# The key sums of an attention step issued directly behind its weighted product, ahead of the step's remaining score tiles

## What is computed

```
x = x + attn(layernorm(x))                 # 8 heads, each a difference of two softmaxes
    scores = q @ k.T                       # 16 score heads of width 16, 1024 x 1024 each
    probs  = softmax(scores)
    diff   = probs[even] - lam * probs[odd]
    attn   = rms_scaled(diff @ v) @ Wo.T
x = x + ffn(layernorm(x))                  # gates: sigmoid, sigmoid, tanh; scan over the 16 batches
```

## Time and profile before

| | |
|---|---|
| time, median of 3 runs | 5260.5 us (5259.5 to 5261.4) |
| time of the profiled execution | 5259.74 us |
| its span | 5257.9 us |
| granted TensorE clock, mean | 0.979 |
| TensorE (PE) busy | 4979.5 us, 95% |
| VectorE (DVE) busy | 4021.4 us, 76% |
| GpSimd (POOL) busy | 2891.7 us, 55% |
| ScalarE (ACT) busy | 2722.8 us, 52% |

### The profile page before, as it was taken

One profiled execution on the slowest core, in us unless ns is written; L12 is line 12 of the kernel. 1 busy time (PEld: TensorE's weight loads), 2 busy tenths in 40 slices (PEclk: granted clock), 3 DMA queues, 4 the chain that ended last, 5 costly groups with the idle time before them and its releaser, 6 DMA issues.

```text
span 5257.9 us, 65030 instructions
## 1 busy us (share of the span) xinstructions
PE 4979.5 (95%) x24784; PEld 1695.8 (32%) x24784; DVE 4021.4 (76%) x6183; ACT 2722.8 (52%) x3173; POOL 2891.7 (55%) x2118
## 2 busy tenths in 40 slices
PE   6999999999999999999999999999999999999999
PEld 2224232332423223242332423233242322323237
DVE  6877777877778877777887777787777887777526
ACT  1464645556465554545556454554546555463652
POOL 3573746647275573727657374664727557372750
PEclk7899999999999999999999999999999999999999
DMA  6031221302222131222303122130222213122117
GB/s 141 26 60 46 50 64 37 69 37 58 52 45 69 33 64 40 45 66 51 67 26 62 45 45 69 34 72 37 54 56 45 69 33 61 43 45 59 65 49 280
DMA packets 127706, 311.05 MB, mean 59 GB/s; under 512 B 27297, under 2 KB 30498, under 8 KB 113442
## 3 DMA queue, kind: packets, MB, share of 16 engines
q1 hardware_dynamic: 124178, 289.33, 23.2%
q10 hardware_dynamic: 3216, 17.57, 0.9%
HBM read 172.07 MB, written 99.61 MB: 52 GB/s over the span
## 4 chain that ended last, share of the span: by engine, by line
PE 64%; DVE 16%; issue 13%; POOL 3%; ACT 3%; DMA 0%; ACTq 0%; POOLq 0%; SPq 0%; DVEq 0%
PE o_ps L792 15%; PE s_ps L749 15%; PE st L777 13%; PE sum_ps L807 8%; DVE neg_max L1043 7%; PE st L891 3%; PE st L735 3%; POOL pair_sum L472 2%; PE st L717 2%; PE st L957 2%; ACT probs L564 2%; DVE stats L983 2%; DVE xa L1026 1%; DVE swapped L1021 1%; PE st L870 1%
## 5 line engine op out<-in xcount | busy, mean ns | idle before, releaser
L472 POOL TENSOR_TENSOR pair_sum<-probs 128x512 f32<-128x512 f32 x2048 | 2795.4, 1398 | 1436.4 <-ACT probs L564 1432.2
L1043 DVE TENSOR_REDUCE neg_max<-s_ps 128x1 f32<-128x512 f32 x4096 | 2679.4, 687 | 817.4 <-PE s_ps L749 810.1
L564 ACT ACTIVATE probs<-st 128x1024 f32<-128x1024 f32 x2048 | 1983.6, 1022 | 1240.9 <-PE st L777 996.0
L749 PE MATMUL s_ps<-k_stack,q_stack 96*128 96x512 bf16 x4096 | 1525.8, 393 | 140.9 <-DVE neg_max L1043 122.7
L777 PE MATMUL st<-q_stack,k_stack 99*128 99x512 bf16 x4096 | 1226.9, 385 | 20.2 <-ACT xa L512 6.6
L792 PE MATMUL o_ps<-probs,values 128*32 128x512 f32 x8192 | 1103.6, 611 | 0.7 <-ACT probs L564 0.7
L749 PEld LDWEIGHTS s_ps<-k_stack,q_stack 96*128 96x128 bf16 x4096 | 371.1, 97 | 1524.3 <-DVE neg_max L1043 1260.6
L777 PEld LDWEIGHTS st<-q_stack,k_stack 99*128 99x128 bf16 x4096 | 348.3, 99 | 792.6 <-ACT probs L564 414.8
L807 PE MATMUL sum_ps<-pair_sum,ones 128*32 128x512 f32 x4096 | 543.4, 602 | 7.7 <-POOL pair_sum L472 5.7
L891 PE MATMUL st<-xt,weights 128*128 128x512 f32 x768 | 381.7, 594 | 11.8 <-ACT xt L521 11.8
L891 PE MATMUL st<-cell_t,weights 128*128 128x512 f32 x768 | 362.9, 592 | 0.0
(11 more groups left out here) (129 smaller groups left out, 2980.3 us busy)
## 6 DMA issues: line engine op xcount, KB each, us to landing
q_stack<-qk_parts SPq DMA_DIRECT2D x384, 128.0 KB, 4.3
k_stack<-qk_parts SPq DMA_DIRECT2D x378, 128.0 KB, 7.0
swapped<-xa SPq DMA_DIRECT2D x128, 256.0 KB, 2.4
qk_parts<-swapped SPq DMA_DIRECT2D x64, 512.0 KB, 2.8
xa<-in_x SPq DMA_DIRECT2D x16, 1024.0 KB, 6.1
qk_parts<-low_part SPq DMA_DIRECT2D x64, 256.0 KB, 3.0
probs<-in_x SPq DMA_DIRECT2D x16, 1024.0 KB, 10.2
x_rows<-probs SPq DMA_DIRECT2D x16, 1024.0 KB, 3.9
```

What stands on the lines that cost most here:

```text
L472: pool.tensor_tensor(pair_sum[q % 2][:, h, :], probs[a % 4][:, h, :], probs[(a + 1) % 4][:, h, :], ALU.add)\
L564: act.activation(probs[kk % 4][:, 2 * hp:2 * hp + 2, :], st[hp][:, :, :], ACT.Exp).then_inc(exp_done, 1)
L749: pe.matmul(s_ps[i % 2][:, :], q_stack[g][0:SROWS, s, t * P:(t + 1) * P], k_stack[g][0:SROWS, s, h * HALF:(h + 1) * HALF], start=True, sto ...
L1043: dve.tensor_reduce(neg_max2[:, at, i % 2:i % 2 + 1], s_ps[i % 2][:, :], AX.X, ALU.max, negate=True).then_inc(max_done, 1)
```

## The change

In every step with key sums, they move from behind the third and fourth score to directly behind the weighted product. The scores from the third on follow the key sums together. Nothing is added or removed, and no other engine's list changes.

```diff
                     if s >= 1:
                         weighted(u, g, s - 1)
-                    for i in todo[2:4]:
-                        score(un, 1 - g, i)
                     if s >= 4 and s % 2 == 0:
                         key_sums(u, g, (s - 4) // 2)
-                    for i in todo[4:]:
+                    for i in todo[2:]:
                         score(un, 1 - g, i)
                 weighted(u, g, STEPS - 1)
                 key_sums(u, g, 14)
```

## The result

The change makes the kernel slower: 5411.5 us (median of 4 runs, 5411.1 to 5412.1) against 5260.0 us in the same session, a ratio of 1.0288 (95% interval 1.0270 to 1.0306). That is 151 us more, where 137 were forecast.

A forecast was written before the change was run, and what follows sets the result against it. TensorE's list was taken to bound the kernel, with places paced by VectorE. Even units +4.56 us (16 units, +73) and odd units +4.39 (15 units, +66) added 139 to 5259.7: 5399, taken as 5397 us, range 5350 to 5430.

The forecast's parts named there:

- The bound, and the gain: TensorE's list sets the time; adjacent weighted product and key sums save 0.22 us in each of 388 steps, 85 us.
- Rival 1: Faster: the held score costs nothing, only the drain of 0.22 us counts, 5175 us; chance 0.04.
- Term (a): Undisturbed five-score steps, nine an even unit, five an odd: score 4 waits for score 2's maximum, +0.50 us each.
- the upper bound: Held scores may not hide the next weight load, 0.07 us each, 15 us; step 10 may be hit too, 8 us.
- Term (b): Step 8 of even units: key sums wait for GpSimd's pair, then the fifth score is held, +0.75 us.
- The sign of being wrong that named pair_sum: Prediction is wrong if TensorE waits for pair_sum outside steps 4 to 8 of even units.
- Term (c): Step 20 of even units, VectorE late: key sums fill the scores' wait, next step gives back 0.28, -0.69 us.
- (d): Odd units, steps 16 to 18: rotary operation behind a later maximum holds step 17's third and fourth scores, +0.40 us.
- (e): Odd units, steps 20 and 21: rotary operation behind a third score, step 21's third score held 1.1, +0.98 us.
- Term (f): Odd units, steps 6 to 14: four rotary operations make VectorE the pace, +0.45 us; step 28 with the next, +0.06.
- rival 3: The clock falls: short waits bring one more low-clock stretch in each iteration, up to +54 us, 5450 us; chance 0.04.
- Rival 2: Paced places absorb more: only five-score steps pay, three- and four-score steps keep their 0.22 us, 5340 us; chance 0.09.

The follow-up runs named there:

- the pair with half maxima: Kernel before and changed kernel, both with row maxima over 256 of the 512 columns of each score tile: 5203.6 us old order, 5233.7 us new.
- the spaced order: Against the kernel before: third score between weighted product and key sums, the later scores behind the key sums; 5318.6 us, ratio 1.0108.
- the kernel with five-score steps alone: Kernel before with the new order only in steps with five scores (250 of the 388 changed steps): 5377.6 us, ratio 1.0222.
- only the short steps: Kernel before with the new order only in steps with three or four scores (138 steps): 5308.4 us, ratio 1.0091.
- step 6 undone: Changed kernel with the old order put back in step 6 of the odd units alone: 5401.7 us, ratio 1.0266 against the kernel before.
- selected: Kernel before with the new order only in step 20 of even units and step 10 of odd ones: 5233.4 us, ratio 0.9946.
- fifth score moved: Selected kernel, fifth score moved to next step in even steps 10, 18, 26 and odd step 26, new order in odd step 18: 5294.9 us, ratio 1.0063.

## Why the prediction was right, and where its terms were off

**The bound, and the gain.** Right. TensorE's list sets the time, and adjacency saves the passages between matmul shapes: 0.22 us read off the trace, 0.23 where nothing hides it (steps 16 and 28 of the odd units, and the pair with half maxima). The two adjacent rows that the 0.88 and 0.98 were read from the earlier trace rows are of step 8 of unit 15 and not of step 12; both have two scores, and the reading holds. Rival 1, the drain alone, is refuted at the point where it would decide: the third score after a pair started 1.18 us after the first, not under 0.66.

**Term (a), the five-score step.** Right in mechanism and size: +0.50 forecast, +0.50 measured, in 9 and 5 steps a unit. The half maxima showed that it follows the maximum's duration (0.27 us shorter, 0.27 less held), and the spaced order that it hangs on the distance of two scores on one buffer. The 0.07 us in the upper bound, for a weight load that a held score does not hide, shows in no run: behind the held score of step 24 the next matmul comes after 0.22 us (2523.07 to 2523.29), as behind one that is not held.

**Term (b), steps 4 to 8 of the even units.** Forecast +0.75, measured +0.49. Steps 4 to 7 lose 0.12, gain 0.12 twice over and cancel. In step 8 the key sums don't wait for GpSimd any more in the changed kernel; instead the third, fourth and fifth score each wait for VectorE. So the working (b) describes the kernel with five-score steps alone (0.65 us of wait for pair_sum, +0.78), and not the changed one, where the changed steps 4 and 6 move VectorE's rotary operations. That GpSimd finishes earlier because fewer of VectorE's operations fall beside its own is likely, but no run isolated it. The sign of being wrong that named pair_sum did not come: its waits are in steps 4 and 6 of the even units (30 of 32), and the other two stand in the kernel before as well.

**Term (c), step 20.** Right: -0.69 forecast, -0.66 measured.

**Terms (d) and (e).** The mechanism is as told, a rotary operation behind a later maximum holds the next step's third and fourth scores; the sizes were 0.54 for 0.40 and 1.24 for 0.98.

**Term (f).** This is the term that was mis-sized, +1.40 for +0.45 (0.95 x 15 = 14 us). The forecast time was missed by as much, 5411.5 for 5397, which is in part luck, since the other misses cancel. Odd units came out 5.8 us longer from the fourth step on, where 4.4 were forecast. Two things. Steps 8 and 9 lost 1.12 instead of about 0.5. And the prediction let step 10 keep its 0.7 us, and did not see that the key sums of step 12 wait for VectorE's `scale` of the sums before them: 0.77 us. The 0.2 us that it had for the pair of step 14 did not come. The wait in step 12 exists in every kernel that has the new order in step 10 and the old plan of scores (changed, only the short steps, step 6 undone, selected, fifth score moved). Putting back a single matmul in step 6 restored steps 8 and 9 completely, so their loss starts at VectorE, whose rotary operation of step 6 started 3.44 us after the step did before and 4.30 us in the changed kernel (unit 15), and is passed on over two steps.

**The rest.** Terms (d) and (e) too small made 6 us and steps 0 to 2 another 3; the even units' 0.21 too large and the iteration's rest took 3 and 5 off again. The clock stayed (0.979 before, 0.980 after), as forecast; rival 3 is out. Its working had misread a row: the wait of 4.1 us is a single one at 4859 us, and the wait at the start of the odd units is 2.7 us. Rival 2, that the paced places absorb, is out: they cost more than forecast.

## What to carry to other kernels

Before moving a block of work together on the engine that bounds, ask who drains the small buffers meanwhile. With two buffers the spacing of every second producer is at least producer-to-consumer latency plus the consumer's time (here 1.18 us: 0.43 until the maximum starts, 0.69 for it, the rest back to TensorE), and work that stood between producers was not in their way but hid that. In these kernels the move paid in steps where the producer was held already, and such steps are found by the idle time in the timeline: 2 of 28 steps gave 16 of the 27 us that the selected kernel gained. Even there a part comes back at the next wait on the other engine, and the idle time made on VectorE, 76% busy, reappeared behind its next fixed block of work.

Before a difference of two kernels is given to a mechanism, add it up by steps. Here three pairs of kernels differed by 11 to 30 us in stretches that no edit touches, and one of them met its forecast by that.

## What the runs showed of the hardware that was not expected

Steps 0 to 2 of an odd unit have the same list in all these kernels but the pieces named above, and take one of three lengths, which follow the granted clock there. The three stretches (from the kernel with five-score steps only; columns: us, busy by engine, granted clock, DMA share, GB/s):

```profile
946.24:956.07 9.83, 7.16 (x42) 2.20 (x39) 8.22 (x14) 5.81 (x6) 2.73 (x3) 1.00 0.97 173
1264.52:1275.94 11.42, 8.74 (x43) 2.37 (x40) 8.31 (x14) 5.81 (x6) 4.31 (x4) 0.85 0.99 169
625.20:637.77 12.57, 9.89 (x42) 2.64 (x39) 8.46 (x14) 5.92 (x6) 4.54 (x4) 0.73 0.99 161
```

At a mean granted clock of 1.00, 0.85 and 0.73 the same three steps take 9.8, 11.4 and 12.6 us. The clock has two levels, 1.2 and 2.4 GHz, and the mean is lower the longer it stays at the lower one. The stretch from the last step of an odd unit to the next unit has two lengths in the same way, 95.4 and 97.1 us with full maxima, at a mean clock of 1.00 and 0.98. In steps 0 to 2 a wait of TensorE for VectorE's maxima stands ahead of the lower clock, 2.7 us long. But it is as long in all 15 odd units of the five-score kernel, five of which kept the full clock, so the wait alone does not decide. The share of the lengths changes from one kernel to the next, and no run isolated what picks them. Both places together took 9 us off the five-score kernel (8 were missing) and make 11 us of the selected kernel's 27, and they hid 30 us between the two kernels with half maxima. So the selected kernel's gain from the reordering itself is 16 us, and the rest may go with the next edit that shifts the units.

VectorE's rotary operations and GpSimd's additions into `pair_sum` do not run side by side, though they touch different buffers. In the kernel before, 195 of the 248 rotary operations with fp32 output start while one of GpSimd's additions has more than 0.15 us to run. Each of the 195 ends 1.08 to 1.09 us after that addition does, and takes 1.4 to 2.3 us in all; the 23 that meet no addition take 1.21 to 1.23 us. An addition that starts during a rotary operation ends 1.12 to 1.14 us after it, and takes 2.0 to 2.3 us instead of 1.27. So up to 1.1 us of a rotary operation's length hangs on when it starts. Steps 6 to 9 of the odd units have four of them, with maxima between, and there the shift of one matmul shows in their lengths: 1.9, 2.3, 2.3 and 2.3 us in the kernel before, 2.3 us each in the changed one, and 1.8, 1.2, 1.8 and 2.1 us in the mean with the spaced scores, where step 10 is 1.68 us shorter with the same list. Which share of the terms (d) to (f) comes from this no run isolated.
